# A recommendation tower on one core: transposes moved behind their unit, the top network a tile later, weights turned a unit at a time

## The reference

```python
z = einsum('bhd,bmd->bhmd', e, x).reshape(b, n * prev, k)   # x = e, then the first layer's output
x = einsum('bpd,pj->bjd', z, W)                             # W0: 1024 x 128, W1: 4096 x 128
out = sum(concat([x1, x2], axis=1), axis=-1)                # 256 numbers a sample
h = relu(concat([out, dense_ctx]) @ W_top1 + b_top1)        # 272 -> 512
h = relu(h @ W_top2 + b_top2)                               # 512 -> 256
y = h @ W_top3                                              # 256 -> 1
```

## Time and profile before

| What | us |
|---|---|
| median of 3 runs (376.47 to 378.57) | 377.5 |
| the profiled execution's own time | 377.52 |
| its span, first to last instruction | 375.7 |
| PE busy | 323.7 (86%) |
| POOL busy (256 gathers) | 252.3 (67%) |
| ACT busy | 233.9 (62%) |
| DVE busy | 203.2 (54%) |

### The profile page before, as it was taken

How to read it: one execution, slowest core, us unless ns; L and a number is a source line. 1 busy time by engine, 2 the same in 40 slices (tenths; PEclk the granted TensorE clock), 3 DMA queues, 4 the chain that set the end, 5 groups by cost and what they waited for, 6 DMA issues and landing times.

```text
span 375.7 us, 11560 instructions
## 1 busy us (share of the span) xinstructions
PE 323.7 (86%) x4680; PEld 298.8 (80%) x4680; DVE 203.2 (54%) x834; ACT 233.9 (62%) x774; POOL 252.3 (67%) x262
## 2 busy tenths in 40 slices
PE   1899936249998999899989998998699879989897
PEld 1677735248998999899989988988698878889797
DVE  4336999933665565555646663655455544554201
ACT  1578566187667766776686667666676557556601
POOL 5777887877777777777777777777777777740000
PEclk9999996699999999999999999999999999999999
DMA  7801001010100010000101000100010001100000
GB/s 220 312 14 16 11 9 16 9 16 14 16 16 16 14 16 16 16 16 15 16 13 17 15 17 15 15 15 15 15 16 14 16 15 17 15 10 2 3 2 0
DMA packets 10773, 9.79 MB, mean 26 GB/s; under 512 B 4664, under 2 KB 8896, under 8 KB 10720
## 3 DMA queue, kind: packets, MB, share of 16 engines
q0 software_dynamic: 8192, 4.21, 7.5%
q1 hardware_dynamic: 2528, 4.84, 3.8%
HBM read 9.03 MB, written 0.00 MB: 24 GB/s over the span
## 4 chain that ended last, share of the span: by engine, by line
POOL 66%; issue 21%; PE 10%; DMA 1%; ACT 1%; POOLq 0%; DVE 0%; SPq 0%
POOL emb L278 66%; PE WA L726 4%; PE M L739 1%; PE PA L687 1%; DMA emb<-in_table,rows 1%; PE QB L698 1%; DMA base<-in_bases 1%; PE M L758 1%; PE M L749 0%; POOLq L81 0%; ACT h L358 0%; PE T L711 0%; PE T L787 0%; PE M L750 0%; PE ET L787 0%
## 5 line engine op out<-in xcount | busy, mean ns | idle before, releaser
L278 POOL DMA_INDIRECT emb<-in_table,rows x256 | 251.6, 983 | 80.4 <-issue 77.8
L726 PE MATMUL WA<-TS,RX 128*128 128x128 f32 x896 | 111.0, 277 | 1.0 <-ACT TS L285 1.0
L726 PEld LDWEIGHTS WA<-TS,RX 128*128 128x128 f32 x896 | 104.6, 192 | 4.1 <-issue 4.0
L584 DVE COPY TS<-T 32x64 f32<-32x64 f32 x256 | 55.5, 217 | 76.7 <-PE T L711 69.7
L285 ACT ACTIVATE eblk<-ET 32x256 f32<-32x256 f32 x128 | 48.7, 380 | 55.3 <-PE ET L674 53.0
L687 PE MATMUL PA<-eblk,zP 128*128 128x132 f32 x512 | 75.0, 282 | 1.9 <-ACT TS L285 1.1
L552 DVE TENSOR_TENSOR zQ<-ET,eT 128x1024 f32<-128x1024 f32 x32 | 39.2, 1225 | 65.2 <-ACT eT L285 65.1
L285 ACT ACTIVATE TS<-T 32x64 f32<-32x64 f32 (+1 forms) x320 | 66.5, 208 | 7.7
L687 PEld LDWEIGHTS PA<-eblk,zP 128*128 128x128 f32 x512 | 66.7, 195 | 2.7 <-ACT TS L285 1.3
L546 DVE TENSOR_TENSOR zP<-ET,eT 128x224 f32<-128x224 f32 (+6 forms) x224 | 47.7, 289 | 0.0
L285 ACT ACTIVATE TS<-PA 128x396 f32<-128x396 f32 (+1 forms) x96 | 44.5, 463 | 2.7 <-PE PA L687 1.6
(11 more groups left out here) (87 smaller groups left out, 290.5 us busy)
## 6 DMA issues: line engine op xcount, KB each, us to landing
emb<-in_table,rows POOLq DMA_INDIRECT x256, 2.4
TS<-in_W SPq DMA_DIRECT2D x8, 256.0 KB, 5.6
wt<-in_W_top SPq DMA_DIRECT2D x2, 512.0 KB, 8.3
y1w<-in_W_rows SPq DMA_DIRECT2D x1, 448.0 KB, 6.7
TS<-in_W_rows SPq DMA_DIRECT2D x1, 448.0 KB, 7.3
sym<-in_W_cols SPq DMA_DIRECT2D x1, 264.0 KB, 3.0
TS<-in_W_cols SPq DMA_DIRECT2D x1, 264.0 KB, 3.3
idc<-in_ids SPq DMA_DIRECT2D x1, 128.0 KB, 2.1
```

Source lines behind the costliest of these rows:

```text
L278: eng.indirect_dma_start(emb[par][:, g, :], None, table, bass.IndirectOffsetOnAxis(rows[:, k, g:g + 1], 0))\
L584: eng.tensor_copy(view(ts[32 * q:32 * q + 32, :, :], P * REST + b0, [[4 * P, 2], [P, 4], [1, 8]]), view(src, q, [[C17, 2], [4, 4], [C33, 8 ...
L726: m = eng.matmul(WA[:, 0:P], C[:, kt, :], TS[k % 2][:, slot_of(kt), :], start=(kt == 0), stop=(kt == KT - 1))
```

## The change

- `emb_transposes(u+1)` stands at the end of unit u, behind its triples, and no longer at its start. Units 0, 1 and 2 are transposed during the products W0 x W1, unit 3 behind unit 1 (`EARLY_AT`, `ahead`).
- `across_triples` now comes first of the three kinds of triples in a unit. The work of the tile before stands ahead of them in one piece (`fill`), where it had been spread between the trios.
- The top network of tile k-2 is done in tile k, a step a unit: `hidden1` in its unit 0, `hidden2` in unit 1, `result` in unit 2. The 56 blocks of `second` are split by `pieces`: 9, 13, 19 and 15 a unit for most tiles; 16, 20, 20 and 0 for tile 6, whose `first` then stands in unit 30, `hidden1` at the end of unit 30, `hidden2` ahead of unit 31, and `result` behind it.
- The weights are turned in place (`C` is gone; `c_slot` points into `RT`, `QC` and `TH`), four calls each in units 4 and 5, five in unit 6 and one in unit 7. The sums are in five parts (`own`, `high`, `low`, `cross`, `rest`), and each four or five calls wait for their part alone.
- ACT copies `ET` to `eT` first (`e_copy`), and the four blocks of `eblk` are copied from `eT` in SBUF. DVE starts its products when `eT` is there, and `eblk` is not waited for.
- The 20 `rest_copies` of a unit: in the first four units DVE does 5 (it did 10), ACT 15; after that 10 each, as before.

The core of the diff:

```diff
@@ tables @@
-        Y2_PER = 7
-        C_AT = SLOTS_TILE - 4
-        C_TO = (0, 3, 6, 10, CB)
-        Y1_AT, L1_AT, L2_AT, Y_AT = 8, 9, 10, 11
+        FIRST_UNIT = ((), (), (), (), (0, 1, 2, 3), (4, 5, 6, 7), (8, 9, 10, 11, 12), (13,))
+        def pieces(k):
+            if k == 0:
+                return (0, 16, 28, 44, KT)
+            if k == END - 1:
+                return (0, 16, 36, KT, KT)
+            return (0, 9, 22, 41, KT)
-        EARLY_AT = (8, 18)
+        EARLY_AT = (10, 20, F - 1)
+        def ahead(u):
+            if u == 1:
+                return 3
+            return u + 1 if 3 <= u < ALL - 1 else None
@@ scalar @@
-                for v in range(NQ):
-                    r = slice(DIM * v, DIM * v + DIM)
...
-                    copy(dst, ET[r, 0:GROUPS * F].rearrange("p (g x h) -> p g x h", x=2, h=HALF)).then_inc(eblk_made, 1)
-                copy(eT[:, :], ET[:, 0:GROUPS * F]).then_inc(eblk_made, 1)
+            def e_copy(u):
+                eng.wait_ge(et_made, u + 1)
+                copy(eT[:, :], ET[:, 0:GROUPS * F]).then_inc(eT_made, 1)
+            def eblk_copy(u, v):
...
+                copy(dst, eT[r, :].rearrange("p (g x h) -> p g x h", x=2, h=HALF)).then_inc(eblk_made, 1)
...
+            for u in range(ALL):
+                k, i = divmod(u, UNITS)
+                mine = list(FIRST_UNIT[u]) if u < len(FIRST_UNIT) else []
+                others = list(range(by_vector(u - 1), NQ)) if u > 0 else []
...
+                if u >= len(EARLY_AT):
+                    e_copy(u)
+                    if 0 < len(mine) < 5:
+                        c_copy(mine.pop(0))
+                    for v in range(NQ):
+                        eblk_copy(u, v)
+                while mine or others:
+                    if mine:
+                        c_copy(mine.pop(0))
+                    if others:
+                        rest_copies(u - 1, others.pop(0))
+                if k >= 2 and i == 0:
+                    hidden1(k - 2)
+                if u == ALL - 1:
+                    hidden1(END - 1)
+                if k >= 1 and i == (2 if k == END else 3):
+                    if k < END:
+                        y1_copy(k - 1)
+                    y2_copy(k - 1)
+                if k >= 2 and i == 2:
+                    y_copy(k - 2)
+                if u == ALL - 2:
+                    y1_copy(END - 1)
+                across_copy(u)
+                for r in range(TRIOS):
+                    part_copy(TRIOS * u + r)
+                if k >= 2 and i == 1:
+                    hidden2(k - 2)
+            hidden2(END - 1)
@@ vector @@
-            own_sums(0)
+            own_firsts(0)
+            own_seconds(0)
+            all_products(1)
             early_sums()
...
+            rest_copies(2, 0)
+            high_sums()
+            for u in range(UNITS, ALL):
+                rest_copies(u - 1, 0)
+                all_products(u)
+                if by_vector(u - 1) > 1:
+                    rest_copies(u - 1, 1)
+                if u == UNITS:
+                    low_sums()
+                    cross_sums()
+                if u == UNITS + 1:
+                    rest_sums()
@@ tensor @@
+            def fill(u):
+                k, i = divmod(u, UNITS)
+                if k >= 2 and i == 0:
+                    hidden1(k - 2)
+                if k >= 2 and i == 1:
+                    hidden2(k - 2)
+                if k >= 2 and i == 2:
+                    result(k - 2)
+                if u == ALL - 1:
+                    hidden2(END - 1)
...
+                    second(k - 1, n0, n1)
+                if n1 == KT and n0 < KT or k == 1 and i == 3:
+                    first(k - 1)
+            for u in range(ALL):
+                fill(u)
+                across_triples(u)
+                for r in range(TRIOS):
+                    triples(TRIOS * u + r)
+                other_triples(u)
+                if u == ALL - 2:
+                    hidden1(END - 1)
+                if ahead(u) is not None:
+                    emb_transposes(ahead(u))
+            result(END - 1)
             last_tile()
```

More of the change, by code:

```diff
@@ L165, in dlrm_cin_tower @@
         et_made = sem("et_made")
+        eT_made = sem("eT_made")
         eblk_made = sem("eblk_made")
@@ L322, in across_copy @@
                 eng.wait_ge(q_made, u + 1)
+                if unit == 0:
+                    wait(eng, y2_made, k - 1)
+                    wait(eng, y1_made, k - 1)
                 for x in range(2):
@@ L378, in _ @@
                     rx_copy(h // 2)
[L379 to L380 removed]
+                for i, at in enumerate(EARLY_AT):
+                    if h == at:
+                        e_copy(i)
+                    if at < h <= at + NQ:
+                        eblk_copy(i, h - at - 1)
             eng.wait_ge(tower_loaded, 16 * 5)
             copy(wt3[:, :, 0], vec[:, N1 + N2:]).then_inc(wt3_made, 1)
[L383 to L405 removed]
@@ L408, in _ @@
+            hidden2(END - 1)
+            for j in range(by_vector(ALL - 1), NQ):
                 rest_copies(ALL - 1, j)
+            y_copy(END - 1)
             y1_copy(END)
@@ L800, in _ @@
                     emb_transposes(EARLY_AT.index(h))
[L801 to L821 removed]
+            def fill(u):
[8 more added lines that the diff above has]
+                    hidden2(END - 1)
+                if k == 0:
+                    return
+                n0, n1 = pieces(k - 1)[i:i + 2]
+                if k == 1:
+                    news = list(FIRST_UNIT[u])
+                    if i == 0:
+                        while news:
+                            weights(news.pop(0))
+                    while n0 < n1 or news:
+                        if news and (4 * W_ORDER.index(W_ORDER[news[0]]) <= n0 + 4 or n0 == n1):
+                            weights(news.pop(0))
+                        if n0 < n1:
+                            second(0, n0, n0 + 4)
+                            n0 += 4
+                else:
+                    second(k - 1, n0, n1)
+                if n1 == KT and n0 < KT or k == 1 and i == 3:
+                    first(k - 1)
```

301 lines of the change are left out of this document (136 added, 165 removed).

## The result

| | median us | runs |
|---|---|---|
| before | 377.11 | 376.47 to 378.57, 4 runs |
| after | 387.86 | 384.06 to 390.37, 4 runs |
| ratio | 1.0246 | 95% interval 1.0162 to 1.033 |

A forecast was written before the change was run, and what follows sets the result against it. The prediction took POOL's gather stream as the clock of the whole run. Its terms, -1.78 at the end, 0 elsewhere and +1.8 for half clock, summed to 0.0: forecast 377.5 us, no change, range 374.7 to 379.8.

The forecast's parts named there:

- The gather stream: POOL's gathers to the last one's start at 332.50: no change, bounds -2 and +3 us, the term with the widest bounds.
- Rival 3: Slower: DVE's adds meet gathers they missed, from 25 to 90 us; with 2.5 us of stretch 380.0 us; chance 0.12.
- The steady part: Units 8 to 27: no cost; PE needs 34.9 us a tile against 40.0 of gathers.
- rival 4: PE does not work off its delay, waiting over 1.1 us in each unit; unit 28 starts late; 380.5 us; chance 0.08.
- Weights in place: Weights turned in place, sums in parts: units 5 and 6 take 9 to 12 us instead of 8.7, nothing at the end.
- Blocks from SBUF: ACT's block copies from SBUF: 417 ns against 380; only four count at the end, 0.16 us.
- Units 28 to 30: PE's work in these units near the end: 10.18, 10.28 and 14.2 us, the last with two small waits.
- Unit 28's start: PE starts unit 28 with its gather, at 304.94 as before.
- The wait for `hidden1`: After unit 31's transposes PE waits for ACT's `hidden1` of tile 6, behind fifteen copies: 5.74 us, before 0.56.
- The clock: TensorE falls to half clock in the wait for `hidden1`, costing 1.8 us on the chain, bounds 0 and 3.
- rival 1: The clock holds at 2.4 GHz in the wait at the end: 375.7 us; chance 0.18.
- the forecast's prices: PE times per piece: transposes 0.27, eight triples 1.90, across and other 1.73, a block of `second` 0.225 us.

The follow-up runs named there:

- r0_after: The changed kernel again, unaltered, in another batch of runs: 386.7 us, ratio 1.020.
- e3_hidden_first: Changed kernel with ACT's `hidden1` of tile 6 moved ahead of `e_copy(31)`, nothing else changed: 380.6 us, ratio 1.008.
- b1_before: The kernel before, unaltered, run once more for a second trace: 380.4 us, one run.
- e1_no_adds: Changed kernel with each DVE add of the weight sums replaced by a memset of the same destination: 373.0 us, ratio 0.986.
- e8_copies: Changed kernel with each DVE add of the sums replaced by a copy of its second operand: 377.2 us, ratio 0.998.
- e2_gaps: Changed kernel with a memset of one spare column behind each DVE add, all adds done: 378.3 us, ratio 1.003.
- e4_before_gaps: The kernel before with a memset of one spare column behind each DVE add of the sums: 369.6 us, ratio 0.980.
- e6_spread: Changed kernel with memsets behind the adds, `hidden1` of tile 6 ahead of `e_copy(31)`, and six blocks of `second` between the trios: 370.1 us, ratio 0.980.
- e5: Changed kernel with a memset behind each add and ACT's `hidden1` of tile 6 ahead of `e_copy(31)`: 372.4 us, ratio 0.987.

## Why the prediction was wrong

**The gather stream (forecast 0, bounds -2 and +3; measured +5.9 and, in r0_after, +7.7).** This term failed, by its size and by the way it was made. The step says "three or four such steps more or less", each of 0.77 us, from eight stretched steps in the earlier trace rows. The size of a hold was taken from a mean in one execution. e3_hidden_first and b1_before show what the unit really is: one gather held for a whole run of adds, up to 7.2 us, in some executions and not in others. The bounds of one profiled execution were taken for the bounds of the kernel. Rival 3 had the cause (e1_no_adds: nothing lost), the place, and the price of 1 us on the last gather for each us of stretch (15.0 - 8.9 = 6.1 lost, 5.9 later). Its size of 2.5 us was too small, and so was its chance of 0.12.

The Trainium skill (SBUF — State Buffer, "SBUF: two separate sides") calls the port pair of DVE and GpSimd an exclusive lock for the whole instruction, and lists two-port modes and two SBUF inputs. That DVE's adds with two SBUF inputs block the gathers agrees with e1_no_adds, and e8_copies agrees with what it says of copies. But from "for the whole instruction" I had concluded that a long add costs a gather the add's remainder. In this case one was held over more than 40 instructions (6.96 us), so that conclusion is wrong here. The measurement decides.

**The steady part (forecast 0).** Half right. PE did work off its delay, waited for gathers again from unit 19 on (221.90), and so nothing of units 4 to 18 reached the end in the profiled run. But the margin was too high: I had 34.9 us of work a tile, and where nothing waits for gathers it is 36.4 (e2_gaps). The kernel before has 36.3 there (e4_before_gaps, units 24 to 28: 263.30 to 299.57), 1.36 of it a wait for ACT's first top layer that the sum of its work had left out; the change removes that wait and makes another. Of the 1.5 us, 4 x 0.28 = 1.1 are triples in one piece, which wait for ACT's part copy of the first trio (`PA`), a cover that the blocks of `second` between the trios had given; e6_spread restores some of it. The delay to be worked off was forecast at 9 to 12 us when PE enters tile 2. It was 10.8 in the profiled run (unit 8's last gather starts at 108.25 and lands 2.4 later, PE transposes it at 121.48), but that was partly luck: the holds had made the gathers late too. PE gets to unit 8 at 118.4 to 126.9 us in all profiles of the changed order, however early the gathers are, so in e2_gaps it is 18.3 behind and in e1_no_adds 22.8. Five tiles at 3.6 us each work off 18. So in e1_no_adds unit 28 still starts 4.8 us behind its gather, the last transposes start 13.0 us after the last gather (322.96 to 335.96), and what rival 4 said of the end is what happens. Its place, PE, was right and its cause, a wait of over 1.1 us in each unit, was not; it needs a quick stream to show.

**Weights in place.** The forecast had units 5 and 6 at 9 to 12 us. Unit 5 takes 11.6, unit 6 takes 12.7 (99.50 to 112.25), unit 7 9.2. Nearly right: 0.7 us over the upper bound. Unit 4, for which it gave no number of its own, takes 21.1 (66.78 to 87.87), with 6.5 us of waits for a sum and for ACT's copies of turned weights and with part of its work at half clock.

**Blocks from SBUF (forecast 417 ns).** 419 ns in 128 copies, on the page. Right.

**Units 28 to 30 (forecast 10.18, 10.28, 14.2).** 10.49, 10.49 and 14.78: +1.1 together. Three times 0.28 are the triples. The waits for `result` and `first` were forecast at 0.3 and 0.7 and cost 0.35 and 0.77 from start to start (the rows give 0.18 and 0.60, as they count from the modelled end of the work before).

**Unit 28's start (forecast: with its gather).** Its last gather starts at 308.36 and with the 2.4 us to landing it could have begun at 310.8. It began at 312.75. The gather of unit 27 was late to land (it started at 298.35, PE had it at 302.21), the clock fell in the wait of 2.35 us, and unit 27 took 10.5 us. That is +1.9. In r0_after unit 27's gather is late as well (300.24 to 303.72), but the clock held at 1.00 through the wait of 1.89, unit 27 took 9.15, and unit 28 started only 0.2 behind its gather. So some 1.4 of the 1.9 are half clock, which the forecast had in one place alone; why a gather lands late is open.

**The wait for `hidden1` (forecast 5.74).** 5.74. Each copy in front of it has the forecast's duration. This was the new wait, it was foreseen in place and size, and e3_hidden_first shows that it and the half clock behind it cost 6.1 us.

**The clock (forecast 1.8).** It fell, rival 1 fell with it. The cost is 2.4: 3.72 - 1.88 on `hidden2` and 1.74 - 1.17 on the products across. With 0.28 for the triples and small waits the end takes 15.37 us from the last transposes to `last_tile`, where the forecast had 12.65 + 1.8 = 14.45: +0.9.

The sum of the profiled executions: 5.9 (stream) + 1.9 (unit 27) + 1.1 (units 28 to 30) + 0.9 (end) = 9.8, and the forecast's own terms were 0.0. `last_tile` moved by 9.85. For r0_after the same terms are 7.7 + 0.2 + 1.1 + 1.1 = 10.1, and it moved by 10.17.

**What the sum hid.** The forecast set -1.78 for work brought ahead of the last gather against a wait. Work brought forward is worth something only where PE would otherwise wait for the gather. The pair with a quiet stream shows it. The transposes of unit 28 on PE in e2_gaps, and in e4_before_gaps:

```profile
301.82 0.44 PE L747 MATMUL ET<-ident,emb 128*128 128x128 f32 x2
```
```profile
299.57 0.38 PE L679 MATMUL ET<-ident,emb 128*128 128x128 f32 x2
```

The changed order is 2.3 us later there, but it has the triples of unit 27 behind it, 3.6 us of work by the forecast's prices, which the kernel before still has ahead. From there to `last_tile` it takes 50.6 us and the kernel before 47.2, that is 3.4 more with 3.6 less to do. So up to unit 28 the new order is 1.4 us ahead, and behind it it loses 7.0, the 5.7 by which `last_tile` is later and those 1.4. With the gathers early, nothing is gained at the end, and the wait and the half clock are lost in full.

Two causes thus stand beside each other, and their sizes don't simply add, as each hides part of the other: ACT's order at the end (6 us, in e3 and in e5) and the held gathers (8.4 us in the changed kernel, 7.5 in the one before, by breaks). How much of the change's loss is a worse meeting of adds and gathers is open: before lost 8.9 and 12.3 us in two profiles, after 15.0 and 17.0 in two and 19.2 in e3_hidden_first. The new places of the adds seem to meet the gathers worse, but no run moves the adds alone, so it is not shown. By the medians it matters little: the writes between the adds win 8.4 us there and 7.5 in the kernel before, 0.9 apart. So the loss reads differently in two accounts. Along the chain of the profiled run the stream is 5.9 of the 9.8 us. With the stream made quiet in both kernels the change still costs 5.6 to 8.7, about 6 of it ACT's order at the end.

## What to carry to other kernels

A stretch that comes from two engines meeting by chance has to be sized by the longest meeting that can be, the whole run of the blocking instructions, and never by the mean of one profile. A second profile of the kernel before can help, but here by its times at most about one execution in six would have shown such a hold: look at the spread of its times too. When DVE works on SBUF for microseconds on end while GpSimd issues indirect DMAs, put a write of one column between its instructions: here that alone made the kernel 2% faster. When a step is moved ahead of a wait, look at every engine's queue: `hidden1` was done on PE, but ACT's copy of it stood behind a wait for something later, and moving one call there was worth 6 us.

## What the runs showed of the hardware

- An indirect DMA of 0.94 us on GpSimd was held for up to 7.2 us while DVE ran adds or fp32 copies with SBUF inputs back to back, and ended 0.82 to 0.83 us behind the last of them in eleven of the fifteen holds of over 2.5 us. In the other four it was let in while they went on. Memsets did not hold it, nor did DVE's copies from PSUM and products of a PSUM with an SBUF operand: from 130 us on, where DVE does only these, no gather of the changed kernel took over 0.96 us.
- Which gather is held, and for how long, differs between executions of one kernel: 2.32 and 7.11 us at the most in two profiles of the kernel before.
- A memset of one column (0.06 us) between the adds cut the lost time from 17.0 to 5.8 us in the changed kernel and to 1.9 and 2.0 in the one before, but one hold of 6.77 was still seen with it (e5_gaps_hidden). What decides whether a gather gets in at a break was not found.
- TensorE's granted clock fell to 0.50 in a wait of 2.35 us with full work ahead of it (before 302.21), held at 1.00 in two of 1.88 and 1.89 in r0_after and through one of 3.35, and fell in the one of 5.74. The length of the wait alone does not order them.
- A gather lands 2.4 us after its start in the median. The last gather of unit 27 took 3.86 us in the changed kernel's profile and 3.48 in r0_after until PE had it.
